# Routing scores of an adaLN block: column-packed score products in the recurrent half

## Chip, cores and metric

One core of one Trainium2 chip runs the whole block. The metric is the time of one execution on the device in microseconds (us), the median of repeated runs. Engine names are those of the profile: PE is the matrix engine, PEld its loading of stationary operands, DVE the vector engine, ACT the scalar engine, POOL and SP the two others.

## What is computed

The input is 4 sequences of 2048 tokens of 256 channels. A gated linear recurrence comes first, then a mixture of 8 experts in which every expert picks 512 of the 2048 tokens of a sequence. The reference, cut to what matters here:

```
h = layernorm(x) * (1 + ca) + sa
x = x + ga * recurrence(h)           # gates, scan over the tokens, W_out
h = layernorm(x) * (1 + cb) + sb
scores = h @ gate_w                  # 256 channels -> 8 experts, float32
probs = softmax(scores); g, m = top_k(probs over the tokens, 512)
x = x + gb * experts(h[m], w1, w2) weighted by g
```

## The kernel before

The 8192 tokens are cut into 16 groups of 512 (4 tiles of 128 tokens), and a loop over stages s = 1 to 16 runs the groups through a pipeline that is written out by hand for each engine. Every engine takes its instructions strictly in the written order and waits on semaphores. A product is named here by its stationary weights. In one stage PE does, in this order:

1. `turned(psT, z1)`: 8 transposes of the normalised rows of group s-1 ("z turn").
2. `turn_x1`: 8 transposes of the rows of group s-4 after the recurrence, into `psX` ("x turn"). ACT copies them to `x1T` (`keep_x1T`).
3. `project`: 8 float32 products of group s-3 with W_out; each is two passes in the trace, so 16.
4. `channels(psA, Wa)`: the product with Wa, 12 passes of 512 columns. It needs both parts of the turned z: ACT makes the high part (`hi_z`), DVE the low part (`lo_z`).
5. `channels(psX, Wx)`: the product with Wx into the bank that the turned x left.
6. `score`: the scores of group s-4: for each of 4 token tiles and 2 halves of the channels a float32 product with 128 stationary columns of `x1T` and 8 moving columns of the score weights `Gb`. The tokens come out on partitions, in `S_tok`.
7. `channels(psA, Wu)`: the third product.

ACT does in a stage `hi_z`, `keep_x1T`, `norm1` of the next group, then waits for Wa and does `gate_a` (a tanh and two exponentials), `gate_x`, a square root between two table loads, and goes on to the next stage's `hi_z`. DVE does `scaled_u`, `gated_input`, `lo_z`, the scan, `add_rows`, two sets of statistics, `clip` and, last, `keep_scores`, which reads the scores.

From stage 8 on DVE also searches, bit by bit, the score threshold of the first sequence: a round is `compare` (DVE counts hits), `count` (PE sums the counts over partitions, a product of one column) and `decide` (DVE). Stages 9 to 15 have four rounds each. PE's four counts stand in the middle of Wa, in the middle of Wx, behind `score`, and in the middle of Wu, and each waits in PE's order for its compare on DVE. PE's z turn waits for the last decision of the stage before. Stage 16 finishes the choice (`sum_ties`, `sum_selected`, `turn_slots` in the same four places). The scores of the last three groups are made behind the loop, and the experts follow: 30 units, PE at work nearly throughout.

Of the kernel before, what the change touches and what calls it, by code (L numbers as in the profile page):

```python
# [6 lines left out]
F32 = mybir.dt.float32  # L7
# [4 lines left out]
ACT = mybir.ActivationFunctionType  # L12
AX = mybir.AxisListType

P = 128
# [33 lines left out]
def adaln_kernel(nc, x, W_in, b_in, W_gx, b_gx, W_ga, b_ga, a_param, W_out, b_out, gate_w, w1, w2, c, wmod, out):  # L49
    B, S, D = x.shape  # L50
    E, _, H = w1.shape
    KD = D // P
# [28 lines left out]
    with keep:  # L81
# [3 lines left out]
        def sem(name):  # L85
            return keep.enter_context(nc.semaphore(name))
# [449 lines left out]
        O_tok = psO[:].rearrange("p h (q d) -> p (h q) d", d=D)  # L536
        S_tok = psT[:, 0, 0:TT * E].rearrange("p (t e) -> p t e", e=E)


# [6 lines left out]
        s_silu = sem("silu_ready")  # L546
        s_spr = sem("silu_spread")
        s_exp = sem("softplus_exp_ready")
# [10 lines left out]
        s_bg = sem("gate_biases_ready")  # L559
        s_sbs = sem("sb_spread")  # L560
        s_sbp = sem("score_bias_in_psum")
# [35 lines left out]
        r_T2 = sem("x1T_in_psum")  # L597
        r_x1T = sem("x1T_ready")
        r_S = sem("scores_in_psum")
        r_sr = sem("scores_scaled")  # L600
# [148 lines left out]
        with nc.Block() as block:  # L749
# [119 lines left out]
            def _(pool):  # L869
# [7 lines left out]

                pool.memset(over_d[:], 1.0 / D).then_inc(s_one, 1)

                def rstd1(g):  # L880
# [123 lines left out]
            def _(act):  # L1004
# [26 lines left out]
                def keep_x1T(g):  # L1031
# [4 lines left out]
                    act.activation(x1T[:], psX[:], ACT.Copy).then_inc(r_x1T, 1)  # L1036

                def norm1(g):

# [116 lines left out]
                for s in range(1, NG + 1):  # L1156
# [13 lines left out]
                    if PAIR_AT <= s < PAIR_AT + 2:  # L1170
                        split_hi(0, s - PAIR_AT)
                    if c_ is not None:
# [52 lines left out]
            def _(dve):  # L1225
# [101 lines left out]
                def keep_scores(g):  # L1327
# [3 lines left out]
                    dve.wait_ge(r_rs2, 2 * g + 2)  # L1331
                    dve.tensor_tensor(s_rs[g % 2][:], S_tok, x1[g % 2][:, :, D + 1:D + 2].to_broadcast([P, TT, E]),
                                      ALU.mult).then_inc(r_sr, 1)
# [86 lines left out]
                def score_weights():  # L1420
# [6 lines left out]
                    dve.tensor_copy(spread_sb[:], sbc[:].rearrange("p b k -> p k b").unsqueeze(3)  # L1427
                                    .to_broadcast([P, KD, B, P])).then_inc(s_sbs, 1)
                    dve.wait_ge(s_w["gate"], 16)
# [5 lines left out]
                def centre_scores():  # L1435
# [5 lines left out]
                    ins.then_inc(s_gw, 1)  # L1441
                    dve.tensor_copy(sb_bc[:], psO[:, 1, 0:B * E].rearrange("p (b e) -> p b e", e=E)).then_inc(s_gw, 1)

                def choice_constants():
# [301 lines left out]
            def _(pe):  # L1746
# [81 lines left out]
                def setup_scores():  # L1828

                    pe.wait_ge(s_sbs, 1)  # L1830
                    pe.wait_ge(s_w["gate"], 16)
# [31 lines left out]
                def turn_x1(g):  # L1863
# [5 lines left out]
                    turned(psX, x1[g % 2]).then_inc(r_T2, 1)  # L1869

                def score(g):

                    pe.wait_ge(r_x1T, g + 1)
                    pe.wait_ge(r_lo, min(g + 4, NG))
                    if g == 0:
                        pe.wait_ge(s_gw, 2)
                    if g >= 1:
                        pe.wait_ge(r_sr, g)
                    for t in range(TT):
# [108 lines left out]
                for s in range(1, NG + 1):  # L1988
# [20 lines left out]
                    if d is not None:  # L2009
                        project(d)  # L2010
                    pe.wait_ge(r_lo, c_ + 1)
                    if c_ == 0:
# [68 lines left out]
```

## Time and profile before

| | |
|---|---|
| Median of 3 runs | 1083.77 us (1083.68 to 1087.53) |
| Span of the profiled execution, first to last instruction | 1092.9 us |
| PE busy in it | 1052.1 us, 96% |
| Mean granted clock of PE | 0.990 of full speed |
| Stages 5 to 16 | about 87 to 277 us of the span |

For the profiled execution the profile gives the span alone, and no time of its own beside it; the span is 9.1 us above the median of the runs. In the rows below, times are us from the span's start; a timeline row is "start, duration, engine, line, operation, result<-operands, tile shape, count, and in brackets the idle time before it with what ended it". Matmuls are pipelined, so the duration of a row of products overlaps the next row; the cost of a row is the distance from its start to the start of the next.

### The profile page before, as it was taken

The numbers are of one execution on the slowest core, as the hardware profiler recorded it, in microseconds if no ns is written. First come the engines' busy times: TensorE is split into PE (matmuls) and PEld (weight loads), VectorE is DVE, ScalarE is ACT, GpSimd is POOL, SyncE is SP. The second block draws the span as 40 slices with busy tenths as digits, with TensorE's granted clock in tenths as the row PEclk, the third lists the DMA queues.
The fourth block names the chain that finished last, engine by engine and source line by source line (L and its number), as shares of the span: only waits on it lengthen the run. The fifth ranks groups of instructions, "written<-read, shape, count | busy, mean of one in ns | idle before, by whom it ended". The sixth has DMA issues, their size and how long they took to land.

```text
span 1092.9 us, 18742 instructions
## 1 busy us (share of the span) xinstructions
PE 1052.1 (96%) x6942; PEld 927.8 (85%) x6942; DVE 726.1 (66%) x1680; ACT 781.1 (71%) x1238; POOL 460.5 (42%) x422
## 2 busy tenths in 40 slices
PE   7989999999999999999999999999999999999985
PEld 6778888888877888899998889999888999888875
DVE  4688999898977888965454554554455554477354
ACT  3668888887677787786567777666777766787741
POOL 2123432331442544354455445444545445454533
PEclk8999999999999999999999999999999999999988
DMA  8057756623349555445234435236453442379650
GB/s 256 3 133 192 228 149 148 155 60 58 85 136 120 123 143 143 117 127 127 40 45 110 100 80 150 45 79 144 85 122 64 93 98 42 75 213 311 172 177 39
DMA packets 96891, 130.85 MB, mean 120 GB/s; under 512 B 17312, under 2 KB 82464, under 8 KB 95776
## 3 DMA queue, kind: packets, MB, share of 16 engines
q1 hardware_dynamic: 62960, 84.11, 24.5%
q0 software_dynamic: 33024, 44.75, 24.2%
q8 instruction: 55, 0.90, 0.4%
q10 hardware_dynamic: 816, 0.79, 0.2%
q14 instruction: 36, 0.29, 0.1%
HBM read 78.96 MB, written 42.27 MB: 111 GB/s over the span
## 4 chain that ended last, share of the span: by engine, by line
PE 78%; DVE 7%; ACT 6%; issue 4%; DMA 2%; POOL 1%; SPq 1%; DVEq 0%; ACTq 0%; POOLq 0%
PE psum L1960 30%; PE psum L1932 30%; PE psum L1751 7%; PE psum L1859 4%; PE psum L1906 2%; PE psum L1770 2%; PE psum L1881 1%; DVE st L1239 1%; PE psum L428 1%; DMA w_raw<-ffn_rows 1%; DVE hs L1303 1%; DMA out_x<-res_t 1%; DVE hit L217 1%; ACT hf L1212 1%; DMA ga_col<-in_L_attn_b_ga 1%
## 5 line engine op out<-in xcount | busy, mean ns | idle before, releaser
L1932 PE MATMUL psum<-w,hidT 128*128 128x256 f32 x3072 | 375.5, 283 | 6.3 <-issue 4.8
L1932 PEld LDWEIGHTS psum<-w,hidT 128*128 128x128 f32 x3072 | 366.5, 190 | 8.6 <-issue 6.5
L1960 PE MATMUL psum<-xT,w 128*128 128x512 f32 x1536 | 370.0, 396 | 2.0 <-DVE xT L1529 1.3
L1542 DVE TENSOR_TENSOR hidT<-hf,hidT 128x512 fp32r<-128x512 f32 x256 | 176.5, 691 | 242.1 <-ACT hidT L1216 237.9
L1960 PEld LDWEIGHTS psum<-xT,w 128*128 128x128 f32 x1536 | 283.5, 188 | 61.7 <-DVE xT L1529 1.7
L960 POOL DMA_INDIRECT ffn_rows<-rows_y,idx_cur x120 | 210.5, 1754 | 228.4 <-issue 181.3
L450 POOL DMA_INDIRECT rows_in<-x_rows,idx_cur x128 | 137.6, 1075 | 169.7 <-DVE idx_cur L421 140.1
L1116 ACT ACTIVATE rows_y<-psum,g_cur 128x256 f32<-128x256 f32 x124 | 51.9, 470 | 164.3 <-PE psum L1932 155.2
L1216 ACT ACTIVATE hidT<-hf 128x512 fp32r<-128x512 f32 x256 | 161.8, 632 | 8.1
L1212 ACT ACTIVATE hf<-psum 128x512 f32<-128x512 f32 x256 | 151.2, 591 | 21.6 <-PE psum L1960 11.1
L410 DVE TENSOR_TENSOR place<-row_id,slot_u 128x1024 bf16<-128x1024 bf16 x64 | 76.3, 1221 | 1.1
L1486 DVE TENSOR_TENSOR w<-w_raw,w 128x1024 fp32r<-128x1024 f32 x60 | 71.5, 1220 | 0.3 <-issue 0.2
L1529 DVE TENSOR_TENSOR xT<-xf,xT 128x1024 fp32r<-128x1024 f32 x32 | 39.2, 1224 | 48.2 <-ACT xT L1106 44.8
L1152 ACT ACTIVATE rows_in<-rows_in 128x256 f32<-128x256 f32 x128 | 66.3, 595 | 3.3 <-DMA rows_in<-x_rows,idx_cur 3.3
L1145 ACT ACTIVATE w<-w_raw 128x1024 fp32r<-128x1024 f32 x60 | 60.0, 1045 | 11.4 <-DMA w_raw<-in_L_ffn_w 11.4
L911 POOL TENSOR_SCALAR ve<-x 128x4 f32<-128x4 f32 x16 | 3.5, 222 | 137.8 <-DVE x L1243 137.8
L1859 PE MATMUL psum<-Wout,hs 128*128 128x256 f32 x256 | 58.1, 380 | 2.4 <-ACT gb_bc L1091 2.4
L1055 ACT ACTIVATE ta<-psum,half_ba 128x512 f32<-128x512 f32 x32 | 20.3, 685 | 52.0 <-PE psum L1751 52.0
L1751 PE MATMUL psum<-hT_z,Wa 128*128 128x512 f32 x192 | 52.7, 422 | 3.4 <-DVE p_t L1280 1.8
L1859 PEld LDWEIGHTS psum<-Wout,hs 128*128 128x128 f32 x256 | 47.4, 190 | 8.4 <-issue 2.6
L1751 PE MATMUL psum<-hT_z,Wu 128*128 128x512 f32 x192 | 50.2, 404 | 0.0
L1751 PE MATMUL psum<-hT_z,Wx 128*128 128x512 f32 x192 | 48.1, 397 | 0.0
(209 smaller groups left out, 1224.9 us busy)
## 6 DMA issues: line engine op xcount, KB each, us to landing
w_raw<-in_L_ffn_w SPq DMA_DIRECT2D x30, 1024.0 KB, 5.8
x_rows<-x SPq DMA_DIRECT2D x16, 516.0 KB, 4.0
x_buf<-in_L_attn_x SPq DMA_DIRECT2D x16, 512.0 KB, 5.9
ffn_rows<-scratch SPq DMA_DIRECT2D x8, 1024.0 KB, 8.6
x_buf<-bias_bc POOLq DMA_DIRECT2D x16, 512.0 KB, 7.8
scratch<-x_rows SPq DMA_DIRECT2D x12, 512.0 KB
out_x<-scratch SPq DMA_DIRECT2D x12, 512.0 KB
w_raw<-ffn_rows SPq DMA_DIRECT2D x12, 512.0 KB
```

What stands on the lines that cost most here:

```text
L410: dve.tensor_tensor(place[n][:, at, :], row_id[:].unsqueeze(1).to_broadcast([P, ST // 2, P]), slot_u[n][:, at, :].to_broadcast([P, ST // 2 ...
L450: pool.indirect_dma_start(rows_in[u % 2][:, t, :], None, xr_dram[b], bass.IndirectOffsetOnAxis(ap=idx_cur[u % 4][:, t:t + 1], axis=0))\
L960: pool.indirect_dma_start(acc_dram[b], bass.IndirectOffsetOnAxis(ap=idx_cur[u % 4][:, t:t + 1], axis=0), rows_y[u % 2][:, t, :], None, com ...
L1152: ins = act.activation(x_u[:, t, 0:D], x_u[:, t, 0:D], ACT.Identity, bias=x_u[:, t, D:D + 1], scale=x_u[:, t, D + 1:D + 2])
L1212: act.activation(hf[m % HF][:], h_bank(u, m), ACT.Gelu_apprx_tanh).then_inc(f_hf, 1)
L1216: act.activation(hidT[0][:, m, :], hf[m % HF][:], ACT.Copy).then_inc(f_hh, 1)
L1486: dve.tensor_tensor(parts[1][:, at, :], raw[:, at, :], parts[0][:, at, :].bitcast(F32), ALU.subtract).then_inc(f_ws, 1)
L1542: dve.tensor_tensor(hidT[1][:, m, :], hf[m % HF][:], hidT[0][:, m, :].bitcast(F32), ALU.subtract).then_inc(f_hl, 1)
L1751: ins = pe.matmul(out_, stationary(qs, k), moving(qm, k), start=(first and j == 0), stop=(last and j == len(terms) - 1))
L1859: ins = pe.matmul(O_tok[:, t, :], hs[d % 2][:, k, t * P:(t + 1) * P], Wout[d // GB % 2][:, k, :], start=(k == 0), stop=(k == KD - 1))
L1932: ins = pe.matmul(y_tile(u, t), hidT[qs][:, k, t * P:(t + 1) * P], w2_s[n % 2][qm][:, k, :], start=(x_ == 0), stop=(x_ == len(terms) - 1))
L1960: ins = pe.matmul(h_bank(u, m), w1_s[n % 2][qs][:, k, m * P:(m + 1) * P], xT[qm][:, k, :], start=(x_ == 0), stop=(x_ == len(terms) - 1))
```

## The change

For the 13 groups whose scores are made inside the loop, `score` is taken out of its place between Wx and Wu. Two steps stand in its stead:

- `score_columns`, between `project` and Wa. Now the score weights are stationary, padded with zeros from 8 to 32 columns, and the turned rows stream: 8 float32 products of 128 moving columns. Each of the 4 token tiles has a group of 32 columns of the array (tile size 128 by 32) and writes 32 partitions of the first bank of `psX`. The loop over the channel halves is outside, the one over the tiles inside.
- `turn_columns`, between Wa and Wx: one transpose of 128 by 128 that brings the tokens back on partitions, in `psT`.

ACT copies the columns from `psX` to SBUF in between (`keep_columns`, behind `norm1`, ahead of `gate_a`). Both new SBUF areas are views of `place`, which the first use of the lists overwrites behind the loop. Setup gains one POOL memset of 256 columns and one DVE copy of 64. The semaphore of the spread bias is merged with another. The scores of the last three groups keep `score`.

```
+                def score_columns(g):
+                    pe.wait_ge(r_x1T, g + 1)
...
+                    for k in range(KD):
+                        for t in range(TT):
+                            ins = pe.matmul(S_cols[t * CG:(t + 1) * CG, :], Gb_cols[:, g // GB, k, :],
+                                            x1T[:, k, t * P:(t + 1) * P], start=(k == 0), stop=(k == KD - 1))
+                    ins.then_inc(r_SC, 1)
+                def turn_columns(g):
+                    pe.wait_ge(r_SC, 2 * g + 2)
+                    if g >= 1:
+                        pe.wait_ge(r_sr, g)
+                    pe.transpose(psT[:, 0, 0:P], s_cols, ident[:]).then_inc(r_S, 1)
...
+                def keep_columns(g):
+                    act.wait_ge(r_SC, 2 * g + 1)
...
+                    act.activation(s_cols, S_cols, ACT.Copy).then_inc(r_SC, 1)
...
                     if d is not None:
                         project(d)
+                    if e_ is not None:
+                        score_columns(e_)
                     pe.wait_ge(r_lo, c_ + 1)
...
                     channels(psA, Wa, n[0], sum_ties if s == NG else None).then_inc(r_A, 1)
                     if e_ is not None:
-                        pe.wait_ge(r_x1T, e_ + 1)
+                        turn_columns(e_)
...
                     channels(psX, Wx, n[1], turn_probs if s == PAIR_AT else None).then_inc(r_X, 1)
-                    if e_ is not None:
-                        score(e_)
```

PE in one search stage before, from the z turn to the first half of Wu (L1770 transposes, L1859 `project`, L1751 Wa, Wx, Wu, L293 `count`, L1881 `score`):

```order
L1770 MATMUL psum<-ident,z_1 128x128 x8
L1770 MATMUL psum<-ident,x_0 128x128 x8
L1859 MATMUL psum<-Wout,hs 128x256 x8
L1751 MATMUL psum<-hT_z,Wa 128x512 x6
L293 MATMUL psum<-n_hit,same_e 128x1
L1751 MATMUL psum<-hT_z,Wa 128x512 x6
L1751 MATMUL psum<-hT_z,Wx 128x512 x6
L293 MATMUL psum<-n_hit,same_e 128x1
L1751 MATMUL psum<-hT_z,Wx 128x512 x6
L1881 MATMUL psum<-Gb,x1T 128x8 x8
L293 MATMUL psum<-n_hit,same_e 128x1
L1751 MATMUL psum<-hT_z,Wu 128x512 x6
```

and the same stretch now, as far as the second count (L1789 transposes, L1878 `project`, L1897 `score_columns`, L1770 Wa, Wx, Wu, L1906 `turn_columns`):

```order
L1789 MATMUL psum<-ident,z_1 128x128 x8
L1789 MATMUL psum<-ident,x_0 128x128 x8
L1878 MATMUL psum<-Wout,hs 128x256 x8
L1897 MATMUL psum<-x1T,place 32x128 x8
L1770 MATMUL psum<-hT_z,Wa 128x512 x6
L293 MATMUL psum<-n_hit,same_e 128x1
L1770 MATMUL psum<-hT_z,Wa 128x512 x6
L1906 MATMUL psum<-ident,place 128x128
L1770 MATMUL psum<-hT_z,Wx 128x512 x6
L293 MATMUL psum<-n_hit,same_e 128x1
```

The score products moved from behind the second count to ahead of Wa and so ahead of the first count; one transpose stands behind Wa.

ACT in the same stage now (L1043 `keep_x1T`, L1058 `norm1`, L1050 `keep_columns`, L1069 the first step of `gate_a`):

```order
L1035 ACTIVATE hT_z<-psum,ca 128x512 x2
L1043 ACTIVATE x1T<-psum 128x1024
L1058 ACTIVATE z_0<-x_buf,nm_0,rs_0 128x256 x4
L1050 ACTIVATE place<-psum 128x128
L1069 ACTIVATE ta<-psum,half_ba 128x512 x2
```

`keep_columns` is the one new row; the rest of ACT's order is as it was.

## Rows read from the trace of the kernel before

**Rows 1.** The page, part 1: busy time, share of the span, instructions.
```profile
PE 1052.1 (96%) x6942; PEld 927.8 (85%) x6942; DVE 726.1 (66%) x1680; ACT 781.1 (71%) x1238; POOL 460.5 (42%) x422
```
**Rows 2.** The line of `score`: duration min/median/max in ns, first and last start.
```profile
L1881 PEld LDWEIGHTS psum<-Gb,x1T x256: 186/192/192, 80.6 to 301.2; 128*128 128x128 f32 x128
```
**Rows 3.** Timeline of PE, stages 5 and 6 (columns as told above).
```profile
87.02 1.06 PE L1770 MATMUL psum<-ident,z 128*128 128x128 f32 x8 [1.50 <-DVE s_rs L1332]
...
92.06 3.14 PE L1751 MATMUL psum<-hT_z,Wa 128*128 128x512 f32 x12
...
104.15 3.62 PE L1859 MATMUL psum<-Wout,hs 128*128 128x256 f32 x16
107.42 3.13 PE L1751 MATMUL psum<-hT_z,Wa 128*128 128x512 f32 x12
...
113.18 1.84 PE L1881 MATMUL psum<-Gb,x1T 128*128 128x8 f32 x16
114.88 3.05 PE L1751 MATMUL psum<-hT_z,Wu 128*128 128x512 f32 x12
117.76 1.04 PE L1770 MATMUL psum<-ident,z 128*128 128x128 f32 x8
```
**Rows 4.** Timeline of ACT, stage 6 to the start of stage 7.
```profile
104.50 1.25 ACT L1028 ACTIVATE hT_z<-psum,ca 128x512 fp32r<-128x512 f32 x2
105.64 1.02 ACT L1036 ACTIVATE x1T<-psum 128x1024 f32<-128x1024 f32 x1
...
110.58 1.27 ACT L1055 ACTIVATE ta<-psum,half_ba 128x512 f32<-128x512 f32 x2 [1.97 <-PE psum L1751]
...
119.85 1.25 ACT L1028 ACTIVATE hT_z<-psum,ca 128x512 fp32r<-128x512 f32 x2
```
**Rows 5.** Timeline of DVE, stage 6: the low part of the turned z.
```profile
105.78 1.41 DVE L1269 SCALAR_TENSOR_TENSOR hT_z<-psum,ca,hT_z 128x512 fp32r<-128x512 f32 x2
```
**Rows 6.** Timeline of PE: fourth counts of stages 8, 13, 14, 15, and stage 14 between.
```profile
147.82 0.18 PE L293 MATMUL psum<-n_hit,same_e 128*128 128x1 bf16 x1 [0.43 <-DVE hit L217]
...
228.00 0.18 PE L293 MATMUL psum<-n_hit,same_e 128*128 128x1 bf16 x1
...
229.51 1.03 PE L1770 MATMUL psum<-ident,z 128*128 128x128 f32 x8
230.38 1.04 PE L1770 MATMUL psum<-ident,x 128*128 128x128 f32 x8
231.25 3.62 PE L1859 MATMUL psum<-Wout,hs 128*128 128x256 f32 x16
234.52 1.74 PE L1751 MATMUL psum<-hT_z,Wa 128*128 128x512 f32 x6
236.10 0.18 PE L293 MATMUL psum<-n_hit,same_e 128*128 128x1 bf16 x1
...
243.81 0.18 PE L293 MATMUL psum<-n_hit,same_e 128*128 128x1 bf16 x1
...
259.55 0.18 PE L293 MATMUL psum<-n_hit,same_e 128*128 128x1 bf16 x1
```
**Rows 7.** Timeline of DVE, stage 14: the first decision, which reads PE's count.
```profile
236.32 0.16 DVE L226 TENSOR_SCALAR flip<-psum 128x1 int32<-128x1 f32 x1
```
**Rows 8.** Windows of DVE, first decision to fourth compare: length, busy (instructions), clock, DMA.
```profile
236.32:243.76 7.44, 7.12 (x33) 1.00 0.11 36
```
**Rows 9.** Timeline of DVE, stage 16: where the chosen slots are read.
```profile
275.50 0.29 DVE L276 TENSOR_SCALAR scratch<-psum 128x128 int32<-128x128 f32 x1 [0.32 <-PE psum L311]
```
**Rows 10.** Timeline of PE: 16 small bf16 products and what starts next.
```profile
281.04 0.55 PE L428 MATMUL psum<-vals_u,place 128*128 128x8 bf16 x16
281.45 0.37 PE L1881 MATMUL psum<-Gb,x1T 128*128 128x8 f32 x2
```
**Rows 11.** The line of `project`: duration min/median/max in ns.
```profile
L1859 PE MATMUL psum<-Wout,hs x256: 379/379/462, 56.6 to 291.7; 128*128 128x256 f32 x128
```
**Rows 12.** Timeline of DVE, stage 3: idle ahead of the low part.
```profile
55.57 1.41 DVE L1269 SCALAR_TENSOR_TENSOR hT_z<-psum,ca,hT_z 128x512 fp32r<-128x512 f32 x2 [0.90 <-ACT hT_z L1028]
```

More of the change, by code:

```diff
@@ L537, in adaln_kernel @@
         S_tok = psT[:, 0, 0:TT * E].rearrange("p (t e) -> p t e", e=E)
+        CG = P // TT
+        S_back = psT[:, 0, 0:P].rearrange("p (t c) -> p t c", c=CG)
+        S_cols = psX[:, 0, 0:P]
+        s_cols = place[0][:].rearrange("p t c -> p (t c)").bitcast(F32)[:, 0:P]
+        Gb_wide = place[1][:].rearrange("p t c -> p (t c)").bitcast(F32)[:, 0:B * KD * CG]
+        Gb_cols = Gb_wide.rearrange("p (b k c) -> p b k c", b=B, k=KD)
         s_c = sem("c_loaded")
@@ L546, in adaln_kernel @@
         s_silu = sem("silu_ready")
-        s_spr = sem("silu_spread")
+        s_spr = sem("silu_then_sb_spread")
         s_exp = sem("softplus_exp_ready")
@@ L559, in adaln_kernel @@
         s_bg = sem("gate_biases_ready")
-        s_sbs = sem("sb_spread")
         s_sbp = sem("score_bias_in_psum")
@@ L598, in adaln_kernel @@
         r_x1T = sem("x1T_ready")
+        r_SC = sem("score_columns_in_psum_then_kept")
         r_S = sem("scores_in_psum")
@@ L878, in _ @@
                 pool.memset(over_d[:], 1.0 / D).then_inc(s_one, 1)
+                pool.memset(Gb_wide, 0.0).then_inc(s_one, 1)
                 def rstd1(g):
@@ L1036, in keep_x1T @@
                     act.activation(x1T[:], psX[:], ACT.Copy).then_inc(r_x1T, 1)
+                def keep_columns(g):
+                    act.wait_ge(r_SC, 2 * g + 1)
+                    if g >= 1:
+                        act.wait_ge(r_S, g)
+                    act.activation(s_cols, S_cols, ACT.Copy).then_inc(r_SC, 1)
                 def norm1(g):
@@ L1171, in _ @@
                         split_hi(0, s - PAIR_AT)
+                    if e_ is not None:
+                        keep_columns(e_)
                     if c_ is not None:
@@ L1331, in keep_scores @@
                     dve.wait_ge(r_rs2, 2 * g + 2)
-                    dve.tensor_tensor(s_rs[g % 2][:], S_tok, x1[g % 2][:, :, D + 1:D + 2].to_broadcast([P, TT, E]),
+                    dve.tensor_tensor(s_rs[g % 2][:], S_back[:, :, 0:E] if g < NG - 3 else S_tok, x1[g % 2][:, :, D + 1:D + 2].to_broadcast([P, TT, E]),
                                       ALU.mult).then_inc(r_sr, 1)
@@ L1427, in score_weights @@
                     dve.tensor_copy(spread_sb[:], sbc[:].rearrange("p b k -> p k b").unsqueeze(3)
-                                    .to_broadcast([P, KD, B, P])).then_inc(s_sbs, 1)
+                                    .to_broadcast([P, KD, B, P])).then_inc(s_spr, 1)
                     dve.wait_ge(s_w["gate"], 16)
@@ L1442, in centre_scores @@
                     dve.tensor_copy(sb_bc[:], psO[:, 1, 0:B * E].rearrange("p (b e) -> p b e", e=E)).then_inc(s_gw, 1)
+                    dve.wait_ge(s_gw, 2)
+                    dve.wait_ge(s_one, 7)
+                    dve.tensor_copy(Gb_cols[:, :, :, 0:E], Gb[:]).then_inc(s_gw, 1)
                 def choice_constants():
@@ L1828, in setup_scores @@
                 def setup_scores():
-                    pe.wait_ge(s_sbs, 1)
+                    pe.wait_ge(s_spr, 2)
                     pe.wait_ge(s_w["gate"], 16)
@@ L1869, in turn_x1 @@
                     turned(psX, x1[g % 2]).then_inc(r_T2, 1)
+                def score_columns(g):
+                    pe.wait_ge(r_x1T, g + 1)
+                    if g == 0:
+                        pe.wait_ge(s_gw, 4)
+                    for k in range(KD):
[5 more added lines that the diff above has]
+                    pe.wait_ge(r_SC, 2 * g + 2)
+                    if g >= 1:
+                        pe.wait_ge(r_sr, g)
+                    pe.transpose(psT[:, 0, 0:P], s_cols, ident[:]).then_inc(r_S, 1)
                 def score(g):
@@ L1874, in score @@
                     pe.wait_ge(r_lo, min(g + 4, NG))
[L1875 to L1878, printed above, removed]
+                    pe.wait_ge(r_sr, g)
                     for t in range(TT):
@@ L2010, in _ @@
                         project(d)
+                    if e_ is not None:
+                        score_columns(e_)
                     pe.wait_ge(r_lo, c_ + 1)
```

## Prediction

> **What bounds the kernel now.** I read the busy table first. PE is busy 96% of the span [rows 1], so work taken from PE looks like time won. But the change touches 13 stages of the recurrence, and there I asked of each stage which wait ends last. The timelines of PE, ACT and DVE, laid beside each other, answer that, and the answer is not PE alone.
>
> In stages 5 to 8 PE runs without a gap, with a period of 15.36 us (Wa at 92.06 and, a stage later, at 107.42 [rows 3]). A second loop is almost as long. ACT starts the high part of z at 104.50 and ends it at 105.75 [rows 4]; DVE makes the low part until 107.19 [rows 5]; Wa could start there and starts at 107.42 [rows 3], 0.23 us later; ACT's gates wait for Wa until 110.58, and from there ACT runs without a pause to the next high part at 119.85 [rows 4]. So PE has to win only about 0.2 us a stage, and then the ACT loop sets the period. **More than that cannot be won here.**
>
> In stages 9 to 15 a third loop goes through the threshold search. From one fourth count on PE to the next: 228.00 to Wa at 234.52 (rest of Wu, z turn, x turn, project) is 6.52 us; to the first count at 236.10 it is 1.58; DVE reads that count at 236.32, 0.22 later [rows 6, 7]; from there DVE works until the fourth compare ends, 7.44 us long and 7.12 of it busy, the rest being gaps between 33 instructions [rows 8]; the next fourth count is at 243.81. The sum is 6.52 + 1.58 + 0.22 + 7.49 = 15.81 us. The seven periods from 147.82 to 259.55 [rows 6] last 111.73 us, 15.96 each: this loop has 0.15 us a stage to spare, and no more. **Wx, score and the first half of Wu are not in it.** They lie beside DVE's 7.49 us. The place between project and Wa is in it.
>
> **The change part by part.**
>
> *Removed: score.* It costs 1.70 us of PE a stage (113.18 to 114.88 [rows 3]), 16 passes of 0.106, paced by loading 128 float32 columns [rows 2]. In the search stages that frees PE between the second and the third count; PE then waits for the fourth compare, which comes no earlier. Gain on the path: the 0.15 us of spare, and nothing else.
>
> *Added: score_columns.* Call T the time that it puts between the end of project and the start of Wa. No array of 32 columns is in this trace, so T is bounded from rows. Passes: 8 products, 16 passes as in score. A float32 pass of 128 moving columns costs 0.109 us (a turn of 8 is 230.38 - 229.51 = 0.87 [rows 6]); half of a project pass (3.27 / 16 = 0.204 for 256 columns [rows 6]) is 0.102. Low end: 16 of the smallest products follow each other in 281.45 - 281.04 = 0.41 us [rows 10], and four groups at work at once would take 4 x 0.109 = 0.43. High end: one pass after the other, 16 x 0.109 = 1.74, and the array running empty before and behind: a project pass lasts 0.379 but the next starts after 0.204 [rows 11, 6], so 0.175 twice, T = 2.09. Below the low end there is nothing, since 16 passes cannot take less than the shortest 16 seen. In between: the two passes of one product use the same 32 columns and must follow each other, and they are issued as neighbours, so only the second pass of a tile and the first of the next can overlap: 9 x 0.109 = 0.98. I take that and one fill or emptying more, rounded: **T = 1.1**.
>
> By the Trainium skill, "TensorEngine Tiling (Array Packing)", section Theoretical Speedup, 32 columns allow up to fourfold speed, but its section Key Properties says that changing the tiling mode drains the array, which speaks against a short packed stretch between full-width products. No run here shows either yet; both together would make T an estimated 0.43 + 0.35 = 0.78.
>
> *What T does in stages 5 to 7.* Stage 5: the z turn waits for DVE's scores at 87.02, Wa follows project at 92.06 [rows 3]; Wa comes T later. Stages 6 and 7: score_columns waits for x1T, which ends at 106.66, 0.76 before Wa [rows 4, 3]; ACT carries the delay of the stage before into x1T unchanged, so each adds T - 0.76. Stage 4 delays ACT by about half a microsecond, which stage 5's wait for DVE [rows 3] hides. Sum: T + 2(T - 0.76) = 3T - 1.52 = **+1.78 us**.
>
> *What T does in the search.* Score_columns stands behind project and ahead of the first count, so it adds to the third loop in full: the period is 15.81 + T, seven of them are 110.67 + 7T against 111.73: 7T - 1.06 = **+6.64 us**. Its own wait costs nothing here: as in stage 6, where x1T ends 0.76 us ahead of the end of project [rows 4, 3], the turned rows are kept by then. Behind the waiting PE stand Wa, the first count and ACT's gates, and DVE waits for the count.
>
> *Stage 16.* PE reaches the slots earlier, since 1.70 - T - 0.11 is freed ahead of them, and DVE's wait of 0.32 us [rows 9] goes: **-0.32 us**. Next late is DVE itself, then the lists.
>
> *Parts at no cost.* Turn_columns is one of eight turns, 0.11 us, behind Wa: beside DVE's 7.49 us in the search, and ahead of Wx, which ACT reads only after its exponentials in stages 5 to 8; without that cover it would be 13 x 0.11 = 1.4 us. Keep_columns copies 128 columns where x1T's 1024 take 1.02 us; it fits ACT's wait of 1.97 us ahead of the gates [rows 4]. If the wait were gone it would cost up to 13 x 0.3 = 4 us, but Wa comes later now, not earlier. Its price has no nearer row, so I bound it by 0 and 1.02 and take 0. In setup, DVE's copy of 64 columns lies ahead of 0.90 us of idle [rows 12], and POOL's memset runs while the first data load. No DMA is added or moved; SP and POOL keep their order otherwise. The experts behind the loop keep their order too and start later by the sum.
>
> **Sum:** 1.78 + 6.64 - 0.32 = +8.1 us, in general 10T - 2.9 (for T over about 0.75). It is made against the profiled span of 1092.9 us, which becomes 1101.0; I carry the difference to the median of the runs, 1083.77, and forecast **1091.9 us** (+0.75%). A measurement of this kernel can tell about 0.5%, 5.4 us, from no change; by the sum that is T = 0.83.
>
> **Rivals.**
>
> 1. *Four groups really run at once.* T = 0.43 to 0.8. At T = 0.5 stage 5 gives +0.5, stages 6 and 7 win back 0.23 each because Wa then follows the low part, the search gives 3.5 - 1.06 = 2.44, stage 16 -0.32: +2.2 us, **1086.0**, within 0.5%. For it: the products of neighbouring tiles use different columns. Against it: the two neighbouring passes of one product do not. This is the packing rule of the Trainium skill's tiling page, section Theoretical Speedup.
> 2. *The change does not do what it says:* the groups run one after the other and the array empties at both ends, T = 2.0. 10 x 2.0 - 2.9 = +17.1 us, **1100.9**. For it: in no row do two float32 products share the array. Against it: the tiles are declared as 128 by 32.
> 3. *PE is the bound in all 13 stages and the saving reaches the end.* Each stage then shortens by 1.70 - T - 0.11 = 0.49 us at T = 1.1: -6.4 us, **1077.4**, faster by over 0.5%. It decides wherever PE never waits for a compare. For it: PE is busy 96% [rows 1], and PE runs through the fourth count of stages 13 to 15 without idle [rows 6]. Against it: DVE's 7.44 us without a pause between the first decision and the fourth compare [rows 8]; PE already waits 0.43 us for a compare in stage 8 [rows 6].
>
> **How the numbers follow.** Forecast, T from 0.83 to 1.5: 0.50. Rival 1: 0.27. Rival 2 and all T over 1.5: 0.19. Rival 3: 0.04. Faster is rival 3, 0.04; same is rival 1, 0.27; slower is the forecast and rival 2, 0.69. The range leaves out rival 3, the lowest of rival 1 and the upper half of rival 2: T = 0.45 gives 1085.4 and T = 1.8 gives 10 x 1.8 - 2.9 = 15.1, 1098.9.
>
> **What would show it.** In the timeline of PE after: project to Wa 3.27 + T instead of 3.27; fourth counts 15.8 + T apart, PE idle ahead of them for DVE's compare, and DVE idle ahead of its first decision for PE's count. The copy of the columns inside ACT's wait for Wa. No gap at the transpose behind Wa. The prediction is wrong if fourth counts lie closer than 15.8 us, if T is outside 0.8 to 1.5, or if the expert half, which I leave as it is, changes its length.

## The result, and the profile after

The changed kernel takes 1091.37 us (median of 6 runs, 1088.73 to 1094.28), the kernel before, measured beside it, 1084.47 us (6 runs, 1083.53 to 1087.53). The ratio of the runs is put at 1.0054 with a 95% interval of 1.0039 to 1.0070 (the two medians alone would give 1.0064): slower by about half a per cent, 4 to 8 us. Its profiled execution took 1088.73 us, with a span of 1086.9. The forecast was 1091.9, and slower.

One caution before the traces are laid side by side. From the first product of the experts to the end, the profiled execution of before took 794.8 us and that of after 783.1, although no line of that half was changed. The same stretch is 783.6 to 786.1 us in all twelve experiment traces below, variants of both kernels. So it is the profiled execution of before that was long there. I therefore compare the two traces only up to the first product of the experts.

The page of after, the busy line of part 1 and the chain of part 4 (shares of the span):

```profile
PE 1036.9 (95%) x6955; PEld 902.8 (83%) x6955; DVE 726.7 (67%) x1681; ACT 783.7 (72%) x1251; POOL 464.3 (43%) x423
...
PE 75%; DVE 11%; ACT 6%; issue 4%; DMA 2%; POOL 1%; SPq 0%; DVEq 0%; ACTq 0%; POOLq 0%
```

Against [rows 1], PE is busy 15.2 us less. Of these, 6.4 lie in the unchanged half, which was long before (770.49 us busy there against 764.04); up to the first product of the experts PE is busy 272.81 us instead of 281.57, 8.8 less, and the kernel is slower all the same. The work of the packed products is indeed short. The line of `score_columns` (duration min/median/max in ns, then first and last start in us, then the forms):

```profile
L1897 PEld LDWEIGHTS psum<-x1T,place x208: 106/110/111, 74.6 to 271.6; 128*32 128x32 f32 x104
L1897 PE MATMUL psum<-x1T,place x208: 272/273/298, 74.6 to 271.7; 128*32 128x128 f32 x104
```

Sixteen passes a stage, as before, each loading for 0.11 us instead of 0.19 [rows 2]. Now one search stage on PE, from one fourth count to the next (the timeline of PE, stage 13):

```profile
216.09 0.18 PE L293 MATMUL psum<-n_hit,same_e 128*128 128x1 bf16 x1 [1.34 <-DVE hit L217]
...
219.35 3.62 PE L1878 MATMUL psum<-Wout,hs 128*128 128x256 f32 x16
222.90 0.64 PE L1897 MATMUL psum<-x1T,place 128*32 128x128 f32 x16
223.47 1.66 PE L1770 MATMUL psum<-hT_z,Wa 128*128 128x512 f32 x6
224.98 0.18 PE L293 MATMUL psum<-n_hit,same_e 128*128 128x1 bf16 x1
...
229.67 0.18 PE L293 MATMUL psum<-n_hit,same_e 128*128 128x1 bf16 x1
229.71 1.63 PE L1770 MATMUL psum<-hT_z,Wu 128*128 128x512 f32 x6
232.69 0.18 PE L293 MATMUL psum<-n_hit,same_e 128*128 128x1 bf16 x1 [1.35 <-DVE hit L217]
```

Project to the packed products is 3.55 us where project to Wa was 3.27 [rows 6]; from there to Wa it is 0.57. So T, the time put between project and Wa, is 0.28 + 0.57 = 0.85 us. The period is 232.69 - 216.09 = 16.60 us. Behind the third count PE runs the first half of Wu and then stands for 1.35 us until DVE's compare: this is most of the time that `score` used to fill, 1.70 us [rows 3].

DVE in the same stage and the one behind it. First its windows from the first decision to the fourth compare (length, busy and instructions of DVE, granted clock, DMA):

```profile
225.19:232.64 7.45, 7.13 (x33) 1.00 0.09 33
```

That is the 7.44 us and 33 instructions of [rows 8] again, though that was stage 14. Then the decisions that wait (timeline of DVE):

```profile
225.19 0.16 DVE L226 TENSOR_SCALAR flip<-psum 128x1 int32<-128x1 f32 x1 [0.47 <-PE psum L293]
...
241.78 0.16 DVE L226 TENSOR_SCALAR flip<-psum 128x1 int32<-128x1 f32 x1 [0.58 <-PE psum L293]
```

DVE now waits for PE's first count, where it did not [rows 7], and PE waits for DVE's fourth compare. Neither engine is full; the loop through both sets the period.

The two copies of ACT's stage 6 (timeline of ACT):

```profile
109.28 0.27 ACT L1050 ACTIVATE place<-psum 128x128 f32<-128x128 f32 x1
111.15 1.27 ACT L1069 ACTIVATE ta<-psum,half_ba 128x512 f32<-128x512 f32 x2 [1.61 <-PE psum L1770]
```

`keep_columns` takes 0.27 us, inside a wait for Wa that was 1.97 [rows 4] and is now 1.61 behind it.

### The profile page after: what moved, and what is told of

Its sections match the earlier page's. It is cut to its first block, busy times and chain, and to the rows that moved or that the text cites. A ratio compares the mean times of both kernels' runs of the same rounds, so it can differ in the third digit from the quotient of the medians.

```text
span 1086.9 us, 18783 instructions
## 1 busy us (share of the span) xinstructions
PE 1036.9 (95%) x6955; PEld 902.8 (83%) x6955; DVE 726.7 (67%) x1681; ACT 783.7 (72%) x1251; POOL 464.3 (43%) x423
## 4 chain that ended last, share of the span: by engine, by line
PE 75%; DVE 11%; ACT 6%; issue 4%; DMA 2%; POOL 1%; SPq 0%; DVEq 0%; ACTq 0%; POOLq 0%
PE psum L1994 30%; PE psum L1966 29%; PE psum L1770 4%; PE psum L1878 4%; DVE st L1255 3%; PE psum L1940 2%; PE psum L1789 2%; DVE x L1331 1%; PE psum L428 1%; DMA w_raw<-ffn_rows 1%; DVE hit L217 1%; DVE hs L1319 1%; ACT hf L1228 1%; ACT L1192 1%; DVE hT_z L1285 1%
## 5 line engine op out<-in xcount | busy, mean ns | idle before, releaser
L1966 PE MATMUL psum<-w,hidT 128*128 128x256 f32 x3072 | 369.2, 281 | 1.7 <-DVE hidT L1561 1.7
L1966 PEld LDWEIGHTS psum<-w,hidT 128*128 128x128 f32 x3072 | 361.9, 189 | 2.4 <-DVE hidT L1561 2.3
L967 POOL DMA_INDIRECT ffn_rows<-rows_y,idx_cur x120 | 213.2, 1777 | 228.1 <-issue 183.0
L1878 PE MATMUL psum<-Wout,hs 128*128 128x256 f32 x256 | 58.1, 380 | 2.4 <-ACT gb_bc L1105 2.4
L1069 ACT ACTIVATE ta<-psum,half_ba 128x512 f32<-128x512 f32 x32 | 20.3, 685 | 51.6 <-PE psum L1770 51.6
L1770 PE MATMUL psum<-hT_z,Wa 128*128 128x512 f32 x192 | 52.0, 419 | 3.7 <-DVE Wu L1358 1.8
L1878 PEld LDWEIGHTS psum<-Wout,hs 128*128 128x128 f32 x256 | 47.4, 190 | 8.3 <-issue 2.6
L1770 PE MATMUL psum<-hT_z,Wu 128*128 128x512 f32 x192 | 50.1, 402 | 0.0
L1770 PE MATMUL psum<-hT_z,Wx 128*128 128x512 f32 x192 | 49.3, 403 | 0.0
```

Source lines behind the costliest of these rows:

```text
L967: pool.indirect_dma_start(acc_dram[b], bass.IndirectOffsetOnAxis(ap=idx_cur[u % 4][:, t:t + 1], axis=0), rows_y[u % 2][:, t, :], None, com ...
L1770: ins = pe.matmul(out_, stationary(qs, k), moving(qm, k), start=(first and j == 0), stop=(last and j == len(terms) - 1))
L1878: ins = pe.matmul(O_tok[:, t, :], hs[d % 2][:, k, t * P:(t + 1) * P], Wout[d // GB % 2][:, k, :], start=(k == 0), stop=(k == KD - 1))
L1966: ins = pe.matmul(y_tile(u, t), hidT[qs][:, k, t * P:(t + 1) * P], w2_s[n % 2][qm][:, k, :], start=(x_ == 0), stop=(x_ == len(terms) - 1))
```

## The experiments

Fourth counts are the ruler in all of them. Seven periods, from the fourth count of stage 8 to that of stage 15, last 111.73 us before [rows 6] and 115.33 after, 149.07 to 264.40.

**Is PE's time worth anything in these stages?** `one_product`:

```
-                    for t in range(TT):
-                        for k in range(KD):
+                    for t in range(TT if g >= NG - 3 else 1):
+                        for k in range(KD) if g >= NG - 3 else (0,):
```

> The kernel before, with one of the eight score products left in each of the 13 stages of the loop (scores of those groups are incomplete); PE loses 14 of 16 passes, 1.49 us a stage, 19.4 us in all, and nothing is put in their place. Theory A (the scores of before lie beside other work, loops through ACT and DVE set the period): fourth counts stay 15.8 to 15.95 us apart in stages 9 to 14, stages 5 to 7 win about 0.2 us each, stage 15, where DVE has less to do, about 0.6: 1 to 3 us faster than before in all. Rival (PE is the bound): 13 x 1.49 = 19 us faster, fourth counts about 14.4 us apart.

Measured: 1087.83 us, 1.0012 of before [1.0001, 1.0022]. The kernel before has lost about 19 us of PE work (14 passes of 0.106 us in 13 stages) and gained nothing. Its periods are 16.14, 16.13, 16.05, 15.85, 16.02, 15.82 and 14.54, against 16.12, 16.14, 16.04, 15.85, 16.03, 15.81 and 15.74 before: the same to 0.02 us in six, and shorter by 1.20 in the seventh. PE stands for 1.34 to 1.36 us ahead of each fourth count but the last; here those of stages 12 and 13 (timeline of PE):

```profile
215.39 0.18 PE L293 MATMUL psum<-n_hit,same_e 128*128 128x1 bf16 x1 [1.36 <-DVE hit L217]
...
231.41 0.18 PE L293 MATMUL psum<-n_hit,same_e 128*128 128x1 bf16 x1 [1.34 <-DVE hit L217]
```

So the loop bounds stages 9 to 14, and PE bounds stage 15 alone. That refutes rival 3 everywhere else, and also the 0.15 us of spare that I let PE win.

The expected 1 to 3 us did not come. In the trace, the fourth count of stage 8 comes at 151.22 instead of 147.82. The timeline of PE and its windows show where most of that lies (in the windows: length, then busy us and instructions of PE, PEld, DVE, ACT, POOL, the granted clock, the DMA share, GB/s):

```profile
81.69 3.02 PE L1751 MATMUL psum<-hT_z,Wu 128*128 128x512 f32 x12
87.77 1.94 PE L1770 MATMUL psum<-ident,z 128*128 128x128 f32 x8 [3.06 <-DVE s_rs L1332]
```

```profile
80.00:84.00 4.00, 4.00 (x20) 3.29 (x19) 3.80 (x19) 3.97 (x7) 2.35 (x6) 1.00 0.00 0
84.00:88.00 4.00, 0.94 (x5) 0.50 (x4) 3.83 (x17) 3.95 (x4) 3.27 (x6) 0.87 0.86 230
88.00:92.00 4.00, 4.00 (x18) 3.88 (x18) 3.35 (x5) 2.11 (x5) 1.07 (x1) 0.50 1.08 354
92.00:96.00 4.00, 4.00 (x16) 3.32 (x15) 2.82 (x3) 2.43 (x5) 0.00 (x0) 0.78 0.47 75
```

PE waits 3.06 us for DVE's scores ahead of stage 5's z turn, against 1.50 before [rows 3], and then runs at a granted clock of 0.50, the 1.2 GHz level, for the whole of 88 to 92 us. The 8 transposes take 1.94 us instead of 1.06. Of the 3.40 us, 0.75 lie ahead of that turn, which starts at 87.77 instead of 87.02. I took this up again below.

**Is the place ahead of Wa the loss?** `columns_late` keeps the packing and puts it back where `score` stood; the turn goes to the middle of Wu and ACT's copy behind `gate_x`:

```
                         project(d)
-                    if e_ is not None:
-                        score_columns(e_)
...
                     channels(psX, Wx, n[1], turn_probs if s == PAIR_AT else None).then_inc(r_X, 1)
+                    if e_ is not None:
+                        score_columns(e_)
...
+                        if m == 0 and back is not None:
+                            turn_columns(back)
...
                         gate_x(c_)
+                        if e_ is not None:
+                            keep_columns(e_)
```

> The changed kernel with the packed products at the place of the old ones, between Wx and Wu, into the bank of the turned z; ACT copies the columns behind gate_x, the turn back stands behind the first half of Wu (behind all of Wu in stages 4 to 7). Products, copy and turn are all still made. Theory A (it is the place between project and Wa that costs): T = 0, fourth counts 15.8 to 16.1 us apart, the time within -1 to +2 us of before. Rival (the packed form itself costs: change of the array's division, copy, turn): stays 5 to 7 us above before.

Measured: 1086.32 us, 1.0001 [0.9990, 1.0012]. The loss is gone; the periods are 16.11, 16.12, 16.20, 15.84, 16.19, 15.82 and 15.57, sum 111.85. Beside DVE's work the packed products, their copy and their turn cost nothing over the `score` that they replace. They show no gain either, to within the 1.2 us of the interval. The clock can hide a small one: the profiled execution, the longest of the ten, reached the fourth count of stage 8 only at 150.92, with a granted clock of 0.57 in 88 to 92 us; three of its runs have a mean clock of 0.990 and take 1087.8 to 1088.8 us, and the other seven, at 0.991 to 0.993, have a median of 1085.1. The price of the change lies in where the products stand, not in what they are.

**How large is T, and does it go through one to one?** `columns_twice` runs the 16 passes twice; `one_group` puts all four token tiles into the first 32 columns, so that nothing can run side by side:

```
-                    for k in range(KD):
+                    for k in [k for _ in range(2) for k in range(KD)]:
```

```
-                    for k in range(KD):
-                        for t in range(TT):
-                            ins = pe.matmul(S_cols[t * CG:(t + 1) * CG, :], Gb_cols[:, g // GB, k, :],
+                    for t in range(TT):
+                        for k in range(KD):
+                            ins = pe.matmul(psX[0:CG, 0, t * P:(t + 1) * P], Gb_cols[:, g // GB, k, :],
```

> The changed kernel with the packed products made twice over at their place; T grows from 0.85 to about 0.85 + 0.46 to 0.57 = 1.3 to 1.42 us. Theory A (T lies in full in the loop of the search): fourth counts of stages 9 to 14 go from 16.60 to 17.05 to 17.17 us apart, PE waits for them as before, and the time rises by 8 to 10 times the added T, 4 to 5.5 us over the changed kernel. Rival (the new place costs by its waits or by the division of the array, not by its length): periods stay near 16.6, the time within 1 us of the changed kernel.

> The changed kernel with all four tiles in the first 32 columns of the array, into 512 columns of 32 partitions (scores of the loop's groups are not the reference's); passes, loads and the division of the array stay. Theory: in the changed kernel four passes run at once, 4 waves of 0.11 us; here each pass follows the other, 16 x 0.11 = 1.74 plus about 0.4 for entering and leaving, T about 2.1 us, fourth counts about 17.9 us apart. Rival (a pass of 32 stationary columns is short by itself): T stays near 0.85.

The two timelines of PE, of `columns_twice` first, then of `one_group`:

```profile
222.19 3.62 PE L1878 MATMUL psum<-Wout,hs 128*128 128x256 f32 x16
225.74 1.08 PE L1897 MATMUL psum<-x1T,place 128*32 128x128 f32 x32
226.75 1.43 PE L1770 MATMUL psum<-hT_z,Wa 128*128 128x512 f32 x5
```

```profile
229.07 3.62 PE L1878 MATMUL psum<-Wout,hs 128*128 128x256 f32 x16
232.62 1.94 PE L1897 MATMUL psum<-x1T,place 128*32 128x128 f32 x16
234.48 0.73 PE L1770 MATMUL psum<-hT_z,Wa 128*128 128x512 f32 x2
```

Twice the passes: 1096.44 us, 1.0099 [1.0082, 1.0116], 4.5 thousandths or 4.9 us over after. T is 226.75 - 222.19 - 3.27 = 1.29, so 16 more passes cost 1.29 - 0.85 = 0.44 us, four times 0.11. That leaves 0.85 - 0.44 = 0.41 us in after that is no pass at all: 0.28 between project's end and the first packed pass, and 0.13 behind the last. The 0.28 goes with what stands ahead. In `columns_late` the same products stand behind the second half of Wx, and 227.82 - 226.25 = 1.57 us lie between the two starts, where `score` before followed after 1.47 to 1.49; that is only 0.1 more (timeline of PE in `columns_late`):

```profile
226.25 1.64 PE L1770 MATMUL psum<-hT_z,Wx 128*128 128x512 f32 x6
227.82 0.64 PE L1899 MATMUL psum<-x1T,place 128*32 128x128 f32 x16
```

The period of `columns_twice` is 17.04, also 0.44 over after's.

In one group: 1106.41 us (one run), T = 234.48 - 229.07 - 3.27 = 2.14 and a period of 17.88. Here the 16 passes, with the 0.13 us of leaving, take 1.86 us; less the 0.13 that is 1.73, or 0.108 a pass, one after the other. So in after four passes really share the array, and the packing takes 1.29 us off its own products (1.86 to 0.57). Across after, `columns_twice` and `one_group` the period less T is 15.75, 15.75 and 15.74: T goes into the period one to one.

**Can the loop be loosened?** `count_ahead` moves the first count from the middle of Wa to the place ahead of it:

```
-                    channels(psA, Wa, n[0], sum_ties if s == NG else None).then_inc(r_A, 1)
+                    count(n[0])
+                    channels(psA, Wa, None, sum_ties if s == NG else None).then_inc(r_A, 1)
```

> The changed kernel with the first count ahead of Wa instead of in the middle of it, directly behind score_columns. Theory A: PE takes the count 1.5 us earlier, so DVE no longer waits 0.47 to 0.58 us for it; the first-count loop falls to about 15.15, and the next loop, over two stages through project, score_columns, Wa, ACT's square root and DVE's search, sets about 16.3: fourth counts go from 16.60 to 16.2 to 16.4 us apart, 1.5 to 2.5 us faster than the changed kernel. Rival (DVE's wait for the first count is not what passes T on): periods stay at 16.6.

Measured: 1089.33 us, 1.0037 [1.0022, 1.0051], about 2 us under after, though the two intervals overlap; the trace is the surer evidence. The timeline of PE in stage 13:

```profile
214.14 0.18 PE L293 MATMUL psum<-n_hit,same_e 128*128 128x1 bf16 x1 [1.21 <-DVE hit L217]
...
220.95 0.64 PE L1897 MATMUL psum<-x1T,place 128*32 128x128 f32 x16
221.52 0.18 PE L293 MATMUL psum<-n_hit,same_e 128*128 128x1 bf16 x1
...
230.45 0.18 PE L293 MATMUL psum<-n_hit,same_e 128*128 128x1 bf16 x1 [1.28 <-DVE hit L217]
```

The count follows the packed products at once, and the periods sum to 112.59 us instead of 115.33. PE's work is what it was in after; only its order is another.

`late_before`, `late_after` and `late_columns_late` instead move the fourth count back, from the middle of Wu to behind its ninth pass of 12, the third of the second half (`n` is given for that half of Wu alone):

```
                                         stop=(last and j == len(terms) - 1))
+                        if j == 2:
+                            count(n)
...
-                    channels(psA, Wu, n[3], turn_slots if s == NG else None).then_inc(r_U, 1)
+                    channels(psA, Wu, None, turn_slots if s == NG else None, late=n[3]).then_inc(r_U, 1)
```

> The kernel before with the same move of the fourth count. Here PE is busy without a gap for 15.84 us a stage, so it sets the period once the loop of the search is shorter: Theory A expects 15.84 to 15.9 in stages 9 to 14 instead of 16.00, 0 to 1.5 us faster than before. Rival (the search is all that binds): 15.2 a stage, 5 us faster.

> The changed kernel with the fourth count moved back by half of the second half of Wu (behind the ninth of Wu's 12 passes instead of the sixth), nothing else. Theory A: the loop fourth count, rest of Wu, z turn, x turn, project, score_columns, half of Wa, first count, DVE's 7.49 us loses 0.75 us: 15.81 + 0.85 - 0.75 = 15.9, so fourth counts of stages 9 to 14 go from 16.60 to 15.9 to 16.1 us apart (a loop through ACT's square root over two stages stands next at about 16.0), and the time falls by 3 to 4.5 us against the changed kernel. Rival (what costs is the waiting for x1T or for the columns' copy on ACT, or PE's length): no change, since PE's work and those waits stay.

> The packed products at the place of the old ones (as in columns_late) and the fourth count moved back as well. PE's 1.70 us are down to about 0.8 and no longer in the loop of the search, and the loop is 0.75 shorter. Theory A: now neither PE (15.0) nor the first-count loop (15.05) binds; next is the loop over two stages through ACT's gates and square root and DVE's search, with the copy of the columns in it, about 15.6 to 15.75: fourth counts of stages 9 to 14 that far apart, 1.5 to 3 us faster than before in all. Rival (PE's clock falls in the gaps that the freed PE leaves, or another wait takes the place at once): no faster than before.

`late_before`: 1085.57 us, 0.9999 [0.9989, 1.0009], periods down to 15.85 as expected from stage 11 on, but 16.62 and 16.18 in stages 9 and 10; the seven sum to 112.15, no less than the 111.73 of before. `late_columns_late`, with the packing at the old place: 1085.24, 0.9996 [0.9985, 1.0007], periods of 16.59 and 16.12 in stages 9 and 10, then down to 15.74 where up to 15.6 was hoped for, 111.59 in sum. Neither is a measurable gain. `late_after`: 1091.3, 1.0054 [1.0039, 1.0069], nothing under after, where 3 to 4.5 us were expected. Its periods did fall from stage 11 on, to 16.36 and then 16.05, and the sum to 113.89; in stages 9 and 10 they stayed at 16.92 and 16.90 (16.90 and 16.91 in after). There the z turn waits for DVE, which does 1.22 us of other work between the fourth compare and the decision (timeline of PE, stage 9):

```profile
154.33 1.06 PE L1791 MATMUL psum<-ident,z 128*128 128x128 f32 x8 [0.81 <-DVE s_rs L1348]
```

So a fourth count that stands later wins nothing in those two stages. And the profiled execution reached the fourth count of stage 8 at 152.54 instead of 149.07, with PE idle for 3.07 us ahead of stage 5's z turn, a granted clock of 0.60 in 88 to 92 us, and 1.94 us for the turn. That is `one_product` again.

**Did the clock eat those gains?** Three kernels whose trace or time raised the question, and `late_columns_late`, got extra products in the gap, 12 in three of them and 9 in `late_columns_late`:

```
+                    if s == 4:
+                        for _ in range(12):
+                            pe.matmul(psT[:, 1, :], Wu[0][:, 0, 0:P], hT_z[0][:, 0, :], start=True, stop=True)
```

> one_product with 12 extra products of 512 columns (Wu by the high part of z, result unused, about 12 x 0.24 = 2.9 us) behind Wu of stage 4, where PE was idle for 3.06 us ahead of the z turn of stage 5. The scores stay incomplete as in one_product. Theory A: the idle time ahead of that turn let the granted clock fall to 0.50 in 88 to 92 us, and that cost the 3.2 us by which the first fourth count came late; with PE at work the clock stays at 1.00, the 8 transposes take 1.06 instead of 1.94, the fourth count of stage 8 comes near 148 instead of 151.2, and the time falls by about 3 us, to 0.998 of the kernel before. Theory B: the fall is only in the profiled execution, or something else delays the end: the time stays at 1.0012 of before.

> late_after with the same 12 products behind Wu of stage 4 (idle there 3.07 us). Theory A (the clock fall ate the gain of the later fourth count): clock 1.00 in 88 to 92 us, fourth count of stage 8 near 149 instead of 152.5, time 3 us lower, 1.0025 of before. Theory B: unchanged, 1.0054.

> The changed kernel with the same 12 products behind Wu of stage 4 (idle there 3.07 us, no fall in its profiled execution). Theory A, if its other executions do not fall either: unchanged, 1.0054 of before. If the clock falls in most of its other executions, which range over 5.5 us: up to 3 us lower, 1.003, with a narrower range. Theory B: unchanged.

> late_columns_late with 9 such products behind Wu of stage 4 (idle there 2.38 us). Theory A: its profiled execution had no fall, so at most 1 us is to be had: 0.998 to 0.9996 of before. Theory B: unchanged, 0.9996.

The timeline of PE in `one_product_filled`, and its window of 88 to 92 us:

```profile
84.72 2.96 PE L2031 MATMUL psum<-hT_z,Wu 128*128 128x512 f32 x12
87.94 1.06 PE L1770 MATMUL psum<-ident,z 128*128 128x128 f32 x8 [0.26 <-DVE s_rs L1332]
...
148.43 0.18 PE L293 MATMUL psum<-n_hit,same_e 128*128 128x1 bf16 x1 [1.34 <-DVE hit L217]
```

```profile
88.00:92.00 4.00, 4.00 (x27) 3.74 (x28) 3.97 (x7) 3.42 (x7) 1.24 (x1) 1.00 1.07 376
```

The same for `late_after_filled`:

```profile
87.01 1.06 PE L1791 MATMUL psum<-ident,z 128*128 128x128 f32 x8 [0.30 <-DVE s_rs L1348]
...
149.07 0.18 PE L293 MATMUL psum<-n_hit,same_e 128*128 128x1 bf16 x1 [0.64 <-DVE hit L217]
```

```profile
88.00:92.00 4.00, 4.00 (x24) 3.64 (x23) 3.97 (x5) 3.89 (x7) 0.31 (x1) 1.00 1.10 327
```

With 2.9 us of useless work in the gap the clock stays at 1.00 (2.4 GHz), the turn takes 1.06, and the fourth count of stage 8 comes 2.8 us earlier than without in the one and 3.5 in the other. The times follow, by less than that: `one_product_filled` 1085.93, 0.9996 [0.9986, 1.0005] instead of 1.0012; `late_after_filled` 1089.83, 1.0033 [1.0021, 1.0045] instead of 1.0054. Each pair of intervals overlaps, so this rests on the traces more than on the times. That less comes back in the time than in the trace fits a clock that falls in some executions and not in others, and the mean granted clock of each run says so too. It is 0.988 to 0.990 in eight of ten runs of `one_product`, with a median of 1088.1 us, and 0.991 in the other two, which take 1085.9; with the filling, one run of ten is that low. In `late_after` three of four are, in `late_after_filled` one of ten, and of the runs of before that stood beside `one_product` four of 19. A mean over the span does not say where in it the clock fell. `after_filled` is unchanged (1092.07, 1.0053 [1.0034, 1.0073]) and so is `late_columns_late_filled` (1085.38, 0.9996 [0.9986, 1.0007]). Both had no fall in the profiled execution of the kernel without the filling. So a fall in that gap has no measurable part in the loss of after, and with it out of the way `late_after` comes about 2 us under after (intervals that overlap), while `one_product` still wins nothing measurable. Both fillings fall short of what was expected of them, 1.0025 and 0.998.

No version measured beats the kernel before: the intervals of those near it hold 1, but for that of `one_product`, which begins at 1.0001.

## Why the prediction came out right, and which steps did not

**What bounds the kernel: held.** The loop through the search is the bound in stages 9 to 14. Its four pieces after, read from the rows above: fourth count to Wa 223.47 - 216.09 = 7.38 (forecast 6.52 + T), to the first count 1.51, to DVE 0.21, and from there to the fourth count 7.50. The sum is 16.60; 15.81 + 0.85 says 16.66. `columns_late` and `one_product` show the other half of it: beside DVE's work the packed products cost no more than `score` did, and what is removed there gains nothing.

**T: the mis-sized term.** I took 1.1 and it is 0.85, just inside the band of my forecast. The step that failed is "the two passes of one product use the same 32 columns and must follow each other, and they are issued as neighbours, so only the second pass of a tile and the first of the next can overlap: 9 x 0.109 = 0.98". `columns_twice` and `one_group` show four passes sharing the array throughout, 16 of them in 0.44 us. Rival 1 was right in that mechanism. It was wrong in the bound: I gave it T up to 0.8, and the 0.41 us around the passes lifts T to 0.85. That T still fell into the band of the forecast is luck: my passes were 0.54 us too long (0.98 for 0.44), my ends 0.29 too short (0.12 for 0.41), and the band began at 0.83.

The two rules that I cited from the Trainium skill, "TensorEngine Tiling (Array Packing)", meet their measurement here. Its section Theoretical Speedup gives up to fourfold speed for 32 columns: 1.73 us of serial passes against 0.44 of packed ones is 3.9, so the trace agrees. Its section Key Properties says that a change of the tiling mode drains the array, and gives no time: here entering and leaving cost 0.41 us together, almost as much as the packed work; how much of it is the drain, no run here separates, and behind Wx entering cost only 0.1. The estimate of 0.78 from both was nearer than my 1.1.

**Stages 5 to 7: the size held, not each step.** 3T - 1.52 with T = 0.85 is +1.03; the fourth count of stage 8 moved by 149.07 - 147.82 = +1.25. Where the steps are seen (timeline of PE):

```profile
87.01 1.07 PE L1789 MATMUL psum<-ident,z 128*128 128x128 f32 x8 [3.07 <-DVE s_rs L1348]
...
107.48 0.65 PE L1897 MATMUL psum<-x1T,place 128*32 128x128 f32 x16 [0.38 <-ACT x1T L1043]
108.06 3.06 PE L1770 MATMUL psum<-hT_z,Wa 128*128 128x512 f32 x12
...
118.22 1.06 PE L1789 MATMUL psum<-ident,z 128*128 128x128 f32 x8 [1.39 <-DVE s_rs L1348]
```

The z turn of stage 5 starts where it did [rows 3], so stage 4's delay is hidden as I said. In stage 6 the packed products wait for x1T, as I said. In stage 7 they don't: there the z turn has already waited 1.39 us for DVE's scores, which I had not foreseen. Wa comes 0.85, 0.64 and 1.33 us later in stages 5, 6 and 7, where the formula gives 0.85, 0.94 and 1.03. Stage 8, for which the sum has no term, added nothing.

**The search: right in six stages, wrong in the seventh.** I multiplied one stage by seven. Six periods grew by (249.28 - 149.07) - (243.81 - 147.82) = 4.22 us; 6T less six times 0.15 is 4.2. The size is right, the reason for the 0.15 is not: `one_product` shows that PE could not win it. It was never spare. The pieces were all read in stage 14, so their sum, 15.81, is the period of that stage, and 0.15 is only its distance from the mean of seven stages; a spare would show as a wait. One by one the six grew by 0.78, 0.77, 0.56, 0.76, 0.57 and 0.78. T less 0.07 is 0.78, since Wa reaches its first count in 1.51 us behind the packed products and in 1.58 behind project. In the third and the fifth, stages 11 and 13, DVE was late before (timeline of DVE before, stage 13):

```profile
219.29 1.25 DVE L1303 TENSOR_TENSOR_SCAN hs<-a_t,hs,b_t 128x512 f32<-128x512 f32 x1
...
220.51 0.14 DVE L226 TENSOR_SCALAR flip<-psum 128x1 int32<-128x1 f32 x1
```

PE's first count was there at 220.07, and DVE read it 0.44 later, when its scan was over, instead of 0.22. In those two stages 0.2 us of T went into that wait.

The seventh, stage 15, shrank from 15.74 to 15.12. There DVE has its compare done early and waits for PE's count instead (timeline of DVE after):

```profile
264.07 0.08 DVE L217 DVE_READ_ACCUMULATOR hit<-scratch,cand 128x1 bf16 x1
264.07 0.15 DVE L224 TENSOR_SCALAR kept<-cand 128x1 int32<-128x1 int32 x1
264.61 0.16 DVE L226 TENSOR_SCALAR flip<-psum 128x1 int32<-128x1 f32 x1 [0.39 <-PE psum L293]
```

So PE is the bound in that one stage, and there rival 3 is true: 1.70 - 0.85 - 0.11 = 0.74 us were to be had and 0.62 came. That its fourth count has no idle time ahead of it [rows 6] did not tell the stage apart, since those of stages 13 and 14 have none either. The row of before that would have told me is DVE's decision there, which waits for PE (timeline of DVE before, stage 15):

```profile
259.76 0.16 DVE L226 TENSOR_SCALAR flip<-psum 128x1 int32<-128x1 f32 x1 [0.71 <-PE psum L293]
```

The 1.40 us of statistics that DVE makes for the next group in stage 14 (at 240.65) have no group left in stage 15. By my own sign, fourth counts closer than 15.8 us, the prediction is wrong in this stage; the sign was badly chosen, since 15.74 stood there before the change.

**Stage 16: wrong sign.** I forecast -0.32. From the fourth count of stage 15 to the first product of the experts it is 39.37 us after (264.40 to 303.77) and 38.57 before: +0.80. What I named did happen: DVE no longer waits for the slots, and PE now waits for DVE there, 1.21 us. What I left out is ACT (timeline of DVE after):

```profile
267.77 1.41 DVE L1296 SCALAR_TENSOR_TENSOR p_t<-psum,bias_u,sc_t 128x512 f32<-128x512 f32 x2 [2.35 <-ACT sc_t L1100]
```

ACT's gates start behind Wa of stage 15, which T had delayed, so its square root ends 3.3 us behind the fourth count, where it ended 1.9 behind it before. What PE won in stage 15 is given back here. Taken together stages 15 and 16, with what follows up to the experts, are +0.18.

**The sum.** Up to the first product of the experts: 1.25 + 4.22 - 0.62 + 0.80 = +5.65 us (298.12 to 303.77). My formula with the measured T says 10 x 0.85 - 2.9 = +5.6; it is that close because the errors of stages 5 to 8, 15 and 16 cancel. The medians say +6.9, within the interval of +4.2 to +7.6. So the forecast of +8.1 was 1.2 us over the median and just outside the interval, and its T was too long by a quarter of a microsecond, which is 2.5 us in the sum. That the forecast time of 1091.9 lies only 0.5 us over the measured one is in part luck: the kernel before, to whose 1083.77 I had added the sum, was measured 0.7 us longer this time.

**Parts at no cost: held.** The copy of the columns lies in ACT's wait, the turn behind Wa delays no one that ends late, and the expert half kept its length against every trace but the profiled one of before.

**Rivals.** 2 (serial) is what `one_group` builds: T = 2.14 instead of 2.0. The change does what it says. The low end of my range was a slip of 0.1: its parts at T = 0.45 add up to +1.8 us, which is 1085.5.

## What to carry to other kernels

An engine that is busy 96% of the span can still wait in every turn of a loop that goes through another engine: find which stretch of the program stands inside the loop and which beside it, before pricing an edit by the busy time that it saves. Here about 9 us less PE work made the kernel half a per cent slower, because 0.85 us a stage was put inside the loop and what was saved had stood beside it. And multiply a stage by its count only after looking at the last one: in the stage at the end DVE had less to do, and PE took over as the bound.

## What the runs showed of the hardware

- Entering and leaving a stretch of float32 products packed into 32-column groups cost 0.28 + 0.13 us between full-width products, whether 16 or 32 passes stood in it (`after`, `columns_twice`). Behind the second half of Wx entering cost 0.1 (`columns_late`). What the time goes into stays open.
- Work taken from PE can cost its clock. After 3.06 and 3.07 us without work ahead of stage 5's z turn, the granted clock was 0.50 and 0.60 in 88 to 92 us (`one_product`, `late_after`), and after 2.40 us 0.57 (`columns_late`); 8 transposes took 1.94 instead of 1.06. The same 3.07 us in the profiled execution of after brought no fall, nor did 3.08 in `count_ahead`, 2.62 in `columns_twice` and 2.38 in `late_columns_late`. So the length of the gap alone does not decide it; what else does stays open. Useless products in the gap kept the clock at 1.00 in both kernels where it had fallen.
